# Abs-difference decay in PSUM, the product on VectorE and the D/2 diagonal added by GpSimd, in a kernel of eight Mamba-2 block passes

## What is computed

```
zxbcdt = rmsnorm(x) @ Win
z, xBC, dt = split(zxbcdt);  xBC = silu(causal_conv(xBC));  dt = softplus(dt + dt_bias)
cum = cumsum(dt * A, axis=1)
decay = where(l >= s, exp(cum[l] - cum[s]), 0)
scores[l,s,h] = (C[l] . B[s]) * decay * dt[s]
y = scores @ xh + reversed scan + D * xh
out = x + rmsnorm(y * silu(z)) @ Wout
```

## Time and profile before

| what | us |
|---|---|
| median of 3 runs (2942.47 to 2951.99) | 2949.18 |
| profiled execution | 2953.49 |
| its span | 2951.5 |
| one block pass (start of the second to start of the third) | 248.5 |
| its opening, to the first decay matmul | 53.5 |
| its loop and end, from there | 195.0 |

### The profile page before, as it was taken

The page is one execution under the profiler, slowest core; times in us unless marked ns, Lnnn a source line. Parts: engine busy times, 40 slices in busy tenths (PEclk is TensorE's granted clock), DMA queues, the critical chain, the costliest instruction groups (busy, mean ns, idle before and its releaser), DMA issues. The chain is left out here.

```text
span 2951.5 us, 64266 instructions
## 1 busy us (share of the span) xinstructions
PE 2153.9 (73%) x26182; PEld 1100.1 (37%) x26182; DVE 1981.8 (67%) x2779; ACT 1744.2 (59%) x2811; POOL 1079.7 (37%) x827
## 2 busy tenths in 40 slices
PE   4277777776774887698688588658857886885886
PEld 3022222222221553354255245325524542552553
DVE  2587888888877566565666656565765666666564
ACT  1266766766653575477367457536754773674574
POOL 0044444444451343244045235304522531451342
PEclk6588888888896998799799799869978988997998
DMA  4000000000001111110111111011111101111111
GB/s 133 0 0 1 0 1 0 1 0 0 1 0 29 32 34 28 35 33 15 44 38 26 38 27 40 15 31 32 34 36 26 42 15 39 33 25 30 32 34 31
DMA packets 96695, 74.59 MB, mean 25 GB/s; under 512 B 69392, under 2 KB 77584, under 8 KB 95120
## 3 DMA queue, kind: packets, MB, share of 16 engines
q1 hardware_dynamic: 96400, 70.48, 10.0%
HBM read 20.62 MB, written 8.39 MB: 10 GB/s over the span
## 5 line engine op out<-in xcount | busy, mean ns | idle before, releaser
L892 POOL TENSOR_TENSOR SQ<-SQ 128x512 f32<-128x512 f32 x344 | 467.2, 1360 | 708.4 <-ACT SQ L811 425.1
L859 POOL TENSOR_TENSOR Y<-Z 128x512 f32<-128x512 f32 x256 | 330.8, 1292 | 531.6 <-DVE Z L1096 297.7
L807 ACT ACTIVATE O<-bank 128x512 f32<-128x512 f32 x512 | 304.3, 594 | 210.2 <-PE bank L571 207.5
L1293 DVE TENSOR_TENSOR SQ<-bank,O 128x512 f32<-128x512 f32 x344 | 236.2, 689 | 163.8 <-issue 118.8
L571 PE MATMUL bank<-SS,work 32*128 32x512 bf16 x512 | 203.7, 398 | 169.3 <-ACT O L807 168.2
L892 POOL TENSOR_TENSOR SQ<-O,SQ 128x512 f32<-128x512 f32 x168 | 226.9, 1350 | 254.8 <-PE bank L592 185.7
L1096 DVE TENSOR_TENSOR_SCAN Z<-bank,SS 128x512 f32<-128x512 f32 x256 | 311.0, 1215 | 0.5
L536 PE MATMUL bank<-folded_weights,work 128*64 128x128 f32 x4096 | 300.1, 292 | 0.0
L463 PE MATMUL bank<-Y,constants 128*128 128x512 f32 x512 | 295.5, 662 | 6.2 <-DVE bank L1104 4.6
L592 PE MATMUL bank<-folded_weights,work 128*32 128x64 f32 x8192 | 287.3, 230 | 11.3 <-POOL SQ L892 10.8
L512 PE MATMUL bank<-XP,block_weights 128*128 128x512 f32 x256 | 156.9, 725 | 174.3 <-DVE Z L1227 174.3
(11 more groups left out here) (271 smaller groups left out, 3990.2 us busy)
## 6 DMA issues: line engine op xcount, KB each, us to landing
work<-XP SPq DMA_DIRECT2D x256, 134.0 KB
work<-extra SPq DMA_DIRECT2D x768, 8.0 KB
decay_cols_kept<-extra SPq DMA_DIRECT2D x48, 128.0 KB, 1.8
SS<-decay_cols_kept SPq DMA_DIRECT2D x384, 16.0 KB
block_weights<-callw SPq DMA_DIRECT2D x8, 735.0 KB, 4.4
Z<-state_sel SPq DMA_DIRECT2D x1, 2048.0 KB, 13.2
out<-O SPq DMA_DIRECT2D x2, 1024.0 KB, 8.5
constants<-consts SPq DMA_DIRECT2D x1, 1347.5 KB, 6.1
```

The costliest lines, as they stand in the source:

```text
L807: A(D2C[u % 2], bank[2], ACT.Copy).then_inc(sg("d2_copied"), 1)
L859: g.tensor_tensor(hc[t_ % 4], hs[t_ % 4], c_copy[t_ % 4], ALU.mult).then_inc(sg("s1_hc"), 1)
L892: g.tensor_tensor(MM[u % 2].rearrange("p (h l) -> p h l", l=L), DK[u % 3].rearrange("p (h l) -> p h l", l=L), GM[(u // 8) % 2][:, 64 * (u ...
L1293: v.tensor_tensor(DK[u % 3], bank[u % 2], D2C[u % 2], ALU.min).then_inc(sg("decay_least"), 1)
```

## The change

- **Decay.** The least of two differences is written as an absolute value: with G = dA/2, M = F - G (the middle of a step) and C = log dt - G. One matmul (row tile 0) gives M[l] - M[s] in bank u%3, ACT takes its absolute value in PSUM, a second matmul (row tile 1) adds the rest to it in the same bank, and ACT's exponential (scale -1) works in PSUM too. Three quantities are split and not four, the roundings by ACT, the remainders by DVE.
- **Product.** DVE multiplies the decay in PSUM by the scores into one of three `MM`; the minimum and the `D2C` copy are gone.
- **Diagonal.** POOL adds `Dhalf` to `MM` in place of its product, and the eight matmuls per step with the constant are gone from `y`.
- **z.** All sixteen z tiles are projected before the loop and copied to SBUF by ACT; their tanh (into bank 7) and product are done in the loop, two per group, in slots 0 and 1 of it, up to the last group. Bank 7 also takes the second square.
- **Opening.** B/C and x of the first group are projected and gated before the loop. ACT issues six of the row DMAs (those of C for the first group). The stores and loads of M, G are issued as they come ready.
- **Folding.** The weights of the next pass are folded during this one, into a second buffer; those of the first are folded before the passes begin.
- **Scores.** Two matmuls of 32 rows and 64 columns per u, in tiles (0,0) and (32,64), in place of one of 64 rows and 128 columns; B is gated by one instruction, not two.

```diff
+                def distance(u):
+                    ...
+                    if u >= 3:
+                        pe.wait_ge(sg("multiplied"), c * L + u - 2)
+                    decay_matmul(u, 0).then_inc(sg("distances"), 1)
+                def decay_logs(u):
+                    pe.wait_ge(sg("distance_abs"), c * L + u + 1)
+                    decay_matmul(u, 1).then_inc(sg("decay_logs"), 1)
...
                     for hd in range(2):
-                        for by, first_ in ((Dhalf, True), (MM[u % 2], False)):
-                            for h4 in range(4):
+                        for h4 in range(4):
...
+                project_bc(0)
+                project_x(0, 0)
+                project_x(0, 1)
+                for i in range(5, 16):
+                    z(i)
+                pe.wait_ge(sg("z_copied"), c * 16 + 16)
                 for tau in range(FIRST, LAST):
                     if 0 <= tau - 1 < L:
                         y(tau - 1)
+                    if 0 <= tau + 2 < L:
+                        decay_logs(tau + 2)
                     if 0 <= tau + 3 < L:
-                        decay_logs(tau + 3)
+                        distance(tau + 3)
...
# ACT, in the opening
+                tanh_bc(0)
+                tanh_x(0)
+                act.wait_ge(sg("split_C"), c + 1)
+                decay_rows(act, 0, 1, "C")
+                for i in range(5, 16):
+                    copy_z(i)
# ACT, in a slot: first these two, then tanh_x, tanh_bc, tanh of z, squares, Ln and Exp
+                    u = tau + 2
+                        act.wait_ge(sg("decay_logs"), c * L + u + 1)
+                        A(bank[u % 3], bank[u % 3], ACT.Exp, scale=-1.0).then_inc(sg("decay_ready"), 1)
+                    u = tau + 3
+                        act.wait_ge(sg("distances"), c * L + u + 1)
+                        A(bank[u % 3], bank[u % 3], ACT.Abs).then_inc(sg("distance_abs"), 1)
# POOL
+                    g.tensor_tensor(MM[u % 3], MM[u % 3], Dhalf, ALU.add).then_inc(sg("mixed"), 1)
# DVE, in a slot: the product, then gate_z, gate_x, gate_y, gate_b, ...
+                    u = tau + 1
+                        dve.wait_ge(sg("decay_ready"), c * L + u + 1)
+                        v.tensor_tensor(MM[u % 3], bank[u % 3], GM[(u // 8) % 2], ALU.mult)
```

More of the change, by code:

```diff
@@ L217, in program, with decay_rows, z_at, z_due @@
         LAST, FIRST = L + 16, -9
+        def decay_rows(eng, g, k, name):
+            for j in range(3):
+                l0 = 32 * k + 6 + 8 * j
+                for b in range(NB):
+                    rows = slice(16 * g + 8 * b, 16 * g + 8 * b + 8)
+                    eng.dma_start(LHS[g % 2][l0:l0 + 8, :].rearrange("p (u b l) -> p u b l", b=2, l=L)[:, :, b, :],
+                                  SPLIT[name][j][rows, :].rearrange("h (u l) -> h u l", l=L)).then_inc(
+                        sg(f"decay_rows{g % 2}"), 16)
+        def z_at(i):
+            return slice(TOK * (i % 2) + BANK * (i // 2), TOK * (i % 2) + BANK * (i // 2) + BANK)
+        def z_due(tau):
+            i, r = divmod(tau, 8)
+            return 2 * i + r if r < 2 and 0 <= i < 8 else None
         RH, RC = 4, 4
@@ L276, in rows_of_decay @@
[L276 to L282, removed]
+                        sp.wait_ge(sg("decay_logs"), c * L + 8 * (g - 1))
@@ L797, in call, with tanh_x @@
-                for i in range(3):
-                    z(i)
-                act.wait_ge(sg("folded"), c + 1)
+                round_high("G")
+                round_high("M")
+                round_mid("G")
+                round_mid("M")
+                round_high("C")
+                round_mid("C")
+                def tanh_x(k):
+                    act.wait_ge(sg("x_projected"), c * 16 + k + 1)
+                    if k >= 1:
+                        act.wait_ge(sg("x_ready"), c * 16 + k)
+                    A(TX, bank[3], ACT.Tanh, scale=0.5).then_inc(sg("x_tanh"), 1)
@@ L820, in call @@
[L820 to L827 removed]
+                    if k is not None and k > 0:
+                        tanh_x(k)
@@ new lines, in call @@
+                    g = every(tau, 8, -7, NGROUP)
+                    if g is not None and g > 0:
+                        tanh_bc(g)
+                    i = z_due(tau)
+                    if i is not None:
+                        act.wait_ge(sg("z_copied"), c * 16 + 16)
+                        if i >= 1:
+                            act.wait_ge(sg("z_ready"), c * 16 + i)
+                        if i >= 4:
+                            act.wait_ge(sg("scaled"), c * 8 + i // 2 - 1)
+                        A(bank[7], Z2[:, z_at(i)], ACT.Tanh, scale=0.5).then_inc(sg("z_tanh"), 1)
@@ L1141, in call @@
+            for piece in range(8):
+                fold(0, piece)
             def call(m, n, d, c):
```

384 lines of the change are left out of this document (180 added, 204 removed).

## The result

The changed kernel takes 2958.27 us (median of 13 runs, 2957.0 to 2960.59), the kernel before 2949.18 in the 13 runs beside it. The ratio is 1.0034, with an interval of 1.0025 to 1.0043: slower by a third of a per cent. The forecast was 2922, faster. The range of 2860 to 2985 holds the result, but slower by more than 9 us was given only 26 in 100. The profiled execution took 2957.66 us, with a span of 2955.7.

The account below looks back on a forecast made before the run. PE bounds the steady loop now, a ring of four links after. Per pass: opening -5.3, first two groups -12.2, rest +13.4, total -4.1; eight passes -33, folding +5 once: -28, hence 2922 us, range 2860 to 2985.

Parts of the forecast that it names:

- the clock term: Loop: PE may run at half clock after a pause; 1.5 us charged per steady group and each of the first two.
- rival 4: Loop: the new scores gain nothing and stay near 1.9 us; +0.8 per pass, 2960 us; chance 0.11.
- The ring: Steady loop group: four links bound it in place of PE, together 22.3 us at full clock, against 20.9 before.
- (a): Steady group, second matmul of slot 5 to that of slot 7, through ACT's Ln, Exp and table loads: 6.3 us.
- (b): Steady group, PE's work from slot 7 on to slot 1: pairs, x half, `y` and B/C, 4.1 us.
- (c): Steady group, slots 1 to 2: ACT's tanhs, then DVE gates z before x, for which PE waits: 5.5 us.
- (d): Steady group, PE's work in slots 2 to 5, with scores and squares: 6.35 us.
- the first rival, the forecast: Whole kernel: openings and early groups gain more than the ring costs; 2922 us; chance 0.50.
- The second, the clock kept: Granted clock stays at 1.00 after the opening, steady groups 22.3: 2837 us, half of it 2880; chance 0.12 for both.
- The third, half clock through most of (d): PE at half clock through most of (d), and (b) after (a)'s wait: steady group 26.0, 3025 us; chance 0.14.
- The fifth: ACT's DMAs or z at half clock push the first decay matmul to 1211: +1.2 per pass, 2964 us; chance 0.12.
- The sixth: Loop: ACT's absolute value needs its own table, two loads of 1.28 us every step, 4250 us; chance 0.01.

Follow-up runs that it names:

- experiment 1: Changed kernel with DVE gating x and y before z in its slot; 2855.07 us, ratio 0.9681 to the kernel before.
- experiment 7: Changed kernel with the tanh and gate of z left out of the loop (output not the reference's); 2670.85 us, ratio 0.9048 to the kernel before.
- Experiment 2: Changed kernel with PE repeating the `y` just made twelve times per group, ahead of the x wait; 2884.06 us, ratio 0.9769 to the kernel before.
- experiment 10: Changed kernel with the first group's six C row DMAs issued by SP, not ACT; 2966.43 us, ratio 1.0062 to the kernel before.
- experiment 4: Changed kernel with the old scores (64 rows, 128 columns) and B gated by two instructions; 3086.05 us, ratio 1.0464 to the kernel before.
- experiment 3: Changed kernel with the diagonal back on PE in `y` and no sum on POOL; 3033.55 us, ratio 1.0279 to the kernel before.

## Why the prediction was wrong

It was wrong in sign, by 36 us, while nearly every mechanism in it is there. The signs that it named came too: the first decay matmul 48.5 us after the start, groups of 19.6, 21.4 and 24.1, PE behind the x gate for 3.51 us, less PE time, a lower clock, and PE behind POOL for only 20.3 us in all. What failed is the size of the clock term, in a sum whose large terms nearly cancel. Step by step:

**The opening: right.** -5.3 us predicted, -5.0 found in the pass of the earlier trace rows (53.5 to 48.5), with PE resuming z after a pause of 10.65 us. ACT's six row DMAs took 0.72 us each (0.74 taken), and its copies began 3.24 us after its last operation. In the third to eighth pass the gain was 4.6 to 7.8 us. The opening of the changed kernel in its second pass:

```profile
1196.97 3.60 ACTq L218 DMA_DIRECT2D work<-extra  x5
...
1200.62 2.56 ACT L804 ACTIVATE Z<-bank 128x512 f32<-128x512 f32 x5 [3.24 <-issue]
...
1201.27 8.45 PE L523 MATMUL bank<-XP,block_weights 128*128 128x512 f32 x12 [10.65 <-ACT Z L804]
```

The fold was priced at +5 once and took 9.1 us of DVE (886.54 to 895.60). Part of that does not show, since what stands ahead of it ended 5.6 us earlier than in the kernel before (886.5 for 892.1), for which the forecast had no term and no run here gives the reason. The first pass ended 5.0 us later than before (1163.02 for 1158.03), where +0.9 was predicted: its first decay matmul came 2.5 earlier, and its loop took 203.3 us for 195.7.

**The scores: mis-sized to the safe side.** 1.3 taken, 1.07 found, where it was 1.92. Here 32 matmuls in two row tiles of bank 6, which write different halves of its partitions, took 1.15 us, so rival 4 falls. The Trainium skill (TensorEngine Tiling (Array Packing), Restrictions and Gotchas) states that different row tiles cannot use the same PSUM bank at the same time. By that rule the scores would have stayed near 1.9; the measurement decides against it as a price here.

**The ring: right.** Its links can be read between the rows of L579 in the last long fence of the result. (a) 1552.55 to 1559.01 is 6.46, for 6.3. (b) 1559.01 to 1563.13 is 4.12, for 4.1. (c) 1539.04 to 1544.49 is 5.45, for 5.5, with a wait of 3.51 for "about 3.3". (d) 1544.49 to 1552.55 is 8.06, for 6.35. The sum is 24.1. Experiments 1 and 7 show it by taking it away.

**The clock: the step that failed.** The step said that half clock costs up to 1.7 us "as much of that falls where ACT or DVE bound, I take 1.5", and it took the same 1.5 for each of the first two groups. In the steady group nothing of it fell where ACT or DVE bound. All of it is in link (d), where only PE bounds. Bias 0.58 for 0.37, x half 1.97 and 1.42 for 1.09 each, `y` 0.66 for 0.43, pair 0.60 for 0.39: 1.86 us more than at full clock. Without them (d) is 6.2 and the ring 22.2. Experiment 2 holds the clock and brings most groups to 22.2 to 23.0.

The first two groups were mis-sized more. Forecast were 39.8 us, 36.8 of them at full clock; they took 41.0 in this pass, at 0.83 and 0.84, and 43.2 in the first, third and seventh, where the first of them stands at 0.76. Experiment 2 takes 21.9 us off them over the eight passes, and experiment 10 shows the other side (a lower clock, longer groups). The end is a third miss: the last steps with the end took 38.1 for 37.4 in this pass, and 39.6 in four others. That the clock is the cause there is not shown, and one run speaks against it: in experiment 2 these ends take 309.3 us together for 310.9, although their clock rises (0.70 to 0.73 in the changed kernel, 0.73 to 0.86 there). This cause stays open.

**The sum.** All eight passes together, in the profiled executions; the first two groups are counted from the first decay matmul, and groups end with the absolute value that opens the next:

| us, after less before | forecast | measured |
|---|---|---|
| up to the first decay matmul, with the fold | -37.4 | -43.6 |
| first two groups | -97.6 | -79.2 |
| the rest of the loop and the end | +107.2 | +126.9 |
| all | -28 | +4 |

Openings and early groups gained 123 us, and the ring and the end cost 127; so the first rival, the forecast, fell. Of the first line, 5.6 us are the earlier end of what stands ahead, so that line came out beyond its forecast by luck. In the last line but one, steady groups took 7 us more than forecast (959.1 for 952.0) and the ends 12 (310.9 for 299.2). The large terms were off by 17 to 19%, but they were of the size of 100 us and their net was 28. The sum also stood on one pass. That pass changed by -0.8 us, the third rose by 3.4 (250.6 to 254.0) and the fifth fell by 3.7 (274.8 to 271.1). In the third pass the first two groups take 21.5 and 21.7, the first at a clock of 0.76, and the end 1.5 us more than in the second:

```profile
1461.90:1483.40 21.50, 16.38 (x226) 10.31 (x226) 9.61 (x15) 11.74 (x22) 8.41 (x7) 0.76 0.14 33
```

The eighth pass ends at 2933.12 for 2928.92, which is all by which the profiled executions differ. The rest of the miss is about 4 us: I took it that the profiled execution stood 4.3 above the median as it had before, and this one stood 0.6 below.

**The other rivals.** The second, the clock kept, did not happen by itself; experiment 2 made it for the most part, and got 2884, near its half form (2880). The third, half clock through most of (d) and on in (b), decides from 24.5 us a group; steady groups took 23.7 to 24.3. It is real all the same: in experiment 1 PE ran at half clock from 1252.01 to beyond the squares. The fifth fell with the opening. The sixth fell: L856 ran 512 times with a mean of 574 ns and is idle 12.4 us ahead of them in all, which leaves no room for loads of 1.28 us each. The Trainium skill (ScalarE: Activation LUTs, Table sets: the hidden batching unit) says that abs is in every set. This trace agrees: no absolute value needed a load of its own.

**What stays open.** The old scores cost 128 us (experiment 4), while their matmuls account for 0.85 us a group, 54 us in all. Where the rest falls can be read: the clock is lower (0.799 against 0.818 over the span), most of all in the first two groups, which take 49 us more over eight passes. Why these matmuls bring a lower clock is not settled. The 75 us of experiment 3 are more than the ring was thought to let through: its steady groups are 1.7 us longer on the mean, nearly all of the 1.84 that eight steps of 0.23 come to on PE. They alternate, the shorter ones mostly at a clock of 0.93 and the longer ones at 0.87, and why they do was not found. And why the same pauses cost more clock in one group than in the next is open throughout.

## What to carry to other kernels

When a change moves work from one stage to every iteration of another, ask what stands behind it in each in-order queue: a gate of 0.7 us ahead of the one that PE waited for, on an engine 64% busy, cost 103 us, and swapping them was the cheapest edit here. Treat a wait on PE as two costs, its length and the slow matmuls after it, and charge the second in full where PE is next on the path. Where a forecast is the small net of large terms, read more than one iteration of the kind, sum over all of them, and let the error of the largest term, not the net, set the chances.

## What was not expected of the hardware

- Useless matmuls speed a kernel up: 12 repeats of `y` per group gave 74 us, and 4 in each of two slots gave 130 on top of experiment 1 (2855.07 to 2724.73).
- Short pauses can cost more clock than one long one: behind 0.80 and 0.89 us, apart by one pair, PE once stayed at half clock for 17 us (1252 to 1269 in experiment 1, groups at 0.75 and 0.71) and one group earlier for 3.4, while behind one of 3.51 us half clock was over 4 us after PE resumed (the scores at 1550.06 back at 1.15).
- An opening 2.9 us shorter went with a clock of 0.76 for 0.83 in the next 20 us, and nothing was gained (experiment 10).
- Two row tiles of one bank ran 32 matmuls in 1.15 us, where 16 matmuls with twice the rows and twice the columns took 2.00.
